# Loads at the start moved between queues, and one tile's routing products moved behind product 3

## The reference

```python
def block0(x, slot):                    # slot: one of the adapters, per sequence
    c = x @ W0.T + b0 + 2 * ((x @ A[slot]) @ B[slot])        # rank 16
    h = silu(c @ W_gate.T) * (c @ W_up.T)                    # 1376 wide
    return h @ W_down.T

def block1(x, lang):                    # two layers, each: base + two of eight experts
    g1 = top2_softmax(x @ Wr.T + 5 * onehot(lang))
    y = x @ W1.T + 2 * sum_e g1[e] * (x @ A1[e].T) @ B1[e].T
    g2 = renormalised_top2(softmax(y @ Wr2.T))
    return y @ W2.T + b2 + 2 * sum_e g2[e] * (y @ A2[e].T) @ B2[e].T

x = x + block0(x, itok_B_0_23)
x = x + block1(x, itok_B_0_7)
```

## Time and profile before

| | |
|---|---|
| median of three runs | 988.67 us (988.07 to 990.8) |
| the profiled execution: time, span | 988.7 us, 986.9 us |
| TensorE matmuls busy | 979.6 us, 99% of the span |
| VectorE, ScalarE, GpSimd busy | 60%, 47%, 26% |
| TensorE's granted clock | full in every slice of the span |
| DMA over the span | 233 GB/s |

### The profile page before, as it was taken

How to read it: one execution, slowest core, us unless ns; L and a number is a source line. 1 busy time by engine, 2 the same in 40 slices (tenths; PEclk the granted TensorE clock), 3 DMA queues, 4 the chain that set the end, 5 groups by cost and what they waited for, 6 DMA issues and landing times.

```text
span 986.9 us, 14042 instructions
## 1 busy us (share of the span) xinstructions
PE 979.6 (99%) x4787; PEld 829.0 (84%) x4787; DVE 591.9 (60%) x969; ACT 464.3 (47%) x854; POOL 256.5 (26%) x244
## 2 busy tenths in 40 slices
PE   8999999999999999999999999999999999999998
PEld 7888888888888888888888888888888899888886
DVE  5654586788784423596333299233278488786762
ACT  5645566555761333572333374233357264535342
POOL 5232232654400631400531230171140460000000
PEclk9999999999999999999999999999999999999999
DMA  8997866666977976877887786986789650606132
GB/s 279 359 321 285 310 215 233 250 224 246 340 268 257 293 222 196 268 224 259 298 277 197 225 269 235 316 281 194 195 268 324 235 193 22 234 33 224 65 107 86
DMA packets 121487, 230.12 MB, mean 233 GB/s; under 512 B 12613, under 2 KB 12613, under 8 KB 121161
## 3 DMA queue, kind: packets, MB, share of 16 engines
q1 hardware_dynamic: 118880, 220.81, 67.1%
q0 software_dynamic: 2400, 8.41, 2.3%
q10 hardware_dynamic: 136, 0.01, 0.0%
HBM read 165.74 MB, written 63.44 MB: 232 GB/s over the span
## 4 chain that ended last, share of the span: by engine, by line
PE 94%; DVE 2%; DMA 2%; issue 1%; ACT 1%; POOL 0%; DVEq 0%; SPq 0%; ACTq 0%
PE bank L1820 92%; DMA ab<-in_ab_table,row_i 1%; PE bank L1844 1%; PE bank L1981 1%; DMA t_raw<-t_scratch 1%; ACT xs_hi L1126 0%; DMA slot_i<-in_slots 0%; DVE hg L1644 0%; DVE greater L1624 0%; DVE xs_lo L1529 0%; ACT bank L1277 0%; DVE wins L1620 0%; DVE rank L1627 0%; DVE greater L1618 0%; POOL ab L776 0%
## 5 line engine op out<-in xcount | busy, mean ns | idle before, releaser
L1820 PE MATMUL bank<-cop_hi,wring 128*128 128x512 f32 x1234 | 380.7, 389 | 0.3 <-issue 0.3
L1820 PEld LDWEIGHTS bank<-cop_hi,wring 128*128 128x128 f32 x1234 | 231.6, 188 | 49.0 <-ACT bank L1041 0.9
L1820 PE MATMUL bank<-cop_lo,wring 128*128 128x512 f32 x616 | 239.7, 389 | 0.0
L1820 PE MATMUL bank<-op_hi,wring 128*128 128x512 f32 x560 | 173.7, 389 | 0.0
L1472 DVE TENSOR_TENSOR v<-bank,p7s 128x512 f32<-128x512 f32 x44 | 30.4, 691 | 200.3 <-PE bank L1820 200.3
L1820 PEld LDWEIGHTS bank<-cop_lo,wring 128*128 128x128 f32 x616 | 115.6, 188 | 23.9
L1820 PEld LDWEIGHTS bank<-op_hi,wring 128*128 128x128 f32 x560 | 105.1, 188 | 21.9
L1820 PE MATMUL bank<-op_lo,wring 128*128 128x512 f32 x280 | 108.9, 389 | 0.0
L1072 ACT ACTIVATE s<-bank 128x512 f32<-128x512 f32 x44 | 26.3, 597 | 115.7 <-PE bank L1820 115.7
L1458 DVE TENSOR_TENSOR op_lo<-h,op_hi 128x512 fp32r<-128x512 f32 x100 | 72.6, 743 | 3.9 <-ACT op_hi L1029 3.7
L821 POOL TENSOR_TENSOR h_t<-h,h 128x512 f32<-128x512 f32 x20 | 27.6, 1382 | 160.4 <-DVE h L1494 160.4
(11 more groups left out here) (227 smaller groups left out, 1926.0 us busy)
## 6 DMA issues: line engine op xcount, KB each, us to landing
wring<-wgu_scratch SPq DMA_DIRECT2D x231, 256.0 KB, 3.0
wring<-wd_scratch SPq DMA_DIRECT2D x140, 256.0 KB, 5.2
wgu_scratch<-wring SPq DMA_DIRECT2D x77, 256.0 KB, 3.6
x_raw<-in_x SPq DMA_DIRECT2D x32, 256.0 KB, 7.3
c_scratch<-c_out SPq DMA_DIRECT2D x32, 256.0 KB, 2.8
c<-c_scratch SPq DMA_DIRECT2D x32, 256.0 KB, 4.2
xs_raw<-x_scratch SPq DMA_DIRECT2D x16, 512.0 KB, 5.7
out<-res SPq DMA_DIRECT2D x32, 256.0 KB, 2.1
```

The costliest lines, as they stand in the source:

```text
L1820: return e.matmul(out_ap, lhs, rhs, start=start, stop=stop, skip_group_check=True)
```

## The change

Three edits, all of place. The load of `w0_raw[0]` goes from SyncE's list to the head of ScalarE's, where the load of `slot_i` stood. The load of `slot_i` goes to the head of GpSimd's program. In the last stage, `route_x` of the second next tile stands behind product 3 for every u; `route_x` of the first next tile stays where it was. For u = 0 nothing changes there.

```diff
@@ sync_program
         for k in range(KC):
             load_x(0, [k])
-            e.dma_start(w0_raw[:, k, :], w0[:, k, :]).then_inc(w0_in[k], DMA)
+            if k > 0:
+                e.dma_start(w0_raw[:, k, :], w0[:, k, :]).then_inc(w0_in[k], DMA)
@@ pool_program
+        e.dma_start(slot_i[:, :], slots.unsqueeze(1).to_broadcast([GB, R, n_batch // GB])).then_inc(slots_in, DMA)
         e.iota(part_i[:, :], [[0, 1]], base=0, channel_multiplier=1).then_inc(pool_const, 1)
@@ act_program
-        e.dma_start(slot_i[:, :], slots.unsqueeze(1).to_broadcast([GB, R, n_batch // GB])).then_inc(slots_in, DMA)
+        e.dma_start(w0_raw[:, 0, :], w0[:, 0, :]).then_inc(w0_in[0], DMA)
         split_x(0)
@@ pe_program
                     if mp == 0 and more and i == (3 if u == 0 else 4):
                         route_x(a + 2)
+                    if mp == 0 and more and i == 3:
                         route_x(b + 2)
```

## The result

The changed kernel takes 991.52 us (median of 8 runs, 990.26 to 992.07), the kernel before 988.60 (8 runs): the ratio is 1.0025, 95% interval 1.0014 to 1.0036. It is slower by 2.5 us by the ratio and 2.9 by the medians, where 1.4 us less were forecast, and lies outside the range. The profiled execution has 990.77 us with a span of 989.0.

The account below looks back on a forecast made before the run. TensorE, busy 979.6 of 986.9 us, was taken to set the pace behind the start's chain of slots and gathers. Start 0.3 and last stage 1.1 off 988.7 gave 987.3 us (45%), range 986.0 to 989.4 (94%).

Parts of the forecast that it names:

- What bounds the kernel: Whole kernel: TensorE busy 979.6 of 986.9 us; gains only from the 7.3 us left, useless work in front, or late matmuls.
- Part 1: Start, w0's first chunk by ScalarE's queue: first product 0 to 1.03 us earlier, 0.5 taken; alone worth 0 to 0.2.
- the 4.46 of the bound: Start: if x and w0 loads share 197 GB/s, both land at 4.46 us, first product at 6.60, no gain.
- Part 2: Start, slots' numbers by GpSimd: landing 0.1 to 0.5 us earlier; 0.3 taken for the second gather's landing at 13.03.
- Part 3: Last stage, second tile's routing behind product 3: removes two waits for the split of x, gain 2 x 0.55 = 1.1 us.
- The slack behind it: Last stage: transposes that reuse the banks keep 2 us to spare after ScalarE's last copy slips; expected cost nothing.
- Rival 2: Start: GpSimd's transfer slow among large loads, slots at 5.2, second gather at 14.4; kernel 989.0 to 989.6 us; 12%.
- Rival 1: Start gives nothing or 0.4 back, since the DMA backlog sets the gathers' landing; 987.6 to 988.0 us; 20%.
- Rival 3: Start: both limits give way, second queue shortens the slow phase before 5 us, up to 1.0 earlier; 986.6 us; 15%.
- Rival 4: Last stage: the routing move doesn't pay, a new wait of the same size for bank or router; 988.4 us; 8%.

## Why the prediction was wrong

**What bounds the kernel**: right. The time moved with the start and the two late waits and with little else. One more stall belongs to no edit: `ACT bank L1043`, 0.5 us, which ends at 211.8 us, after ScalarE had waited for a load of gate weights and for GpSimd; the profile of the last-stage edit's second timing has one of 0.4 there, with the start of before.

**Part 1**: right in its pessimistic end. Both loads shared the rate; x was split from 4.41, w0's load took 3.8 us from 0.81, both close to the 4.46 of the bound. Where VectorE was free the first product stood at 6.81, against 6.57 before: no gain. I took 0.5 of the 0 to 1.03. The term itself cost nothing; but the part said that ScalarE loses one issue and gains another "at nothing", and the issue that it loses is that of the slots.

**Part 2** is the step that failed, three times over. First the duration: I took 2.5 to 2.8 us for the slots' landing from GpSimd's small loads of the kernel before, whose issues stand at 9.6 us and later. In the place where the edit puts the load it took 5.5. SyncE's last large load had been issued 5.4 us ahead of those rows (at 4.21). Two stretches of the kernel before show what they met; the last two numbers are the DMA share and the GB/s:

```profile
9.60:10.90 1.30, 1.30 (x6) 1.08 (x7) 1.30 (x3) 0.86 (x2) 1.30 (x4) 1.00 1.03 419
11.50:12.00 0.50, 0.50 (x4) 0.42 (x3) 0.00 (x0) 0.05 (x1) 0.03 (x1) 1.00 0.23 62
```

The engines were still full when these loads were issued and nearly idle when they landed (at 12.1 the first): they met the end of the backlog, the slots its beginning. A row from the right place was there: SyncE's w0 load, issued at 1.26 and so only 0.45 us behind the first, needed 3.8 us, and even that is short of 5.5. The issue itself I put at 0.8 to 0.92; it was at 1.36 and lasted 0.82. Second, who waits: I followed `slot_i` to the gather and never asked what stands behind `row_i` in VectorE's list, which is the first split. The earlier trace rows show VectorE idle for 2.23 us ahead of `row_i`; I read that as room, where it was a wait at the head of a list. The run with the other order measures it, clock included, at 2.3 us. Third, the clock: nothing in the prediction says what an idle stretch in front does to the matmuls after it, though nine warm-up matmuls stand in front of the first product.

**Part 3**: right in mechanism and size. 0.56 and 0.54 us in the trace, 1.1 in all; 1.6 and 0.6 us by the ratios of the two timings. The slack behind it held.

**The rivals.** Rival 2 named the mechanism, a GpSimd transfer that waits in the large loads' backlog, and the point from which it decides, a landing later than 4.9 us. The landing was at 6.91. Its price was too small: it had 5.2 for the landing, it priced only the gather (989.0 to 989.6), and with VectorE's order mended that is what was measured, 989.1. That agreement is in part luck: the slots came 3.0 us later and not 1.4, and the gather made good more than half of it. The 2.3 us more are VectorE's list and the clock. Rival 1 gave the backlog as the reason that nothing is gained; it made things worse instead. Alone, both paths took 2.4 us; by the Trainium skill, "DMA: Bandwidth & Descriptors", section "Specifications", GpSimd's has the slower first byte, which these two runs do not show. W0 on ScalarE's queue landed 5.7 us after issue, behind SyncE's loads; with this agrees the Trainium skill, "DMA: Bandwidth & Descriptors", section "Issuing engines are not separate DMA queues", by which loads that different engines start run on the same DMA engines. Rival 3 did not occur. Rival 4 fell.

In numbers: the last-stage edit -1.1 (trace), the late gathers +1.3 (the run with VectorE's order mended, +0.2, less that), VectorE's list with the clock +2.3; together the 2.5 us of the ratio. The last two terms are differences of that ratio and so must close; the check that does not hang on it is the one of the two traces above, 2.2 against 2.1 us.

## What to carry to other kernels

In this start, where many loads are issued at once, a load that was issued later landed much later, and a queue of its own did not help; a small load that others wait for is best issued first, and moving it from the head of one list to another cost 2.5 us and more, where its issue came 0.46 to 0.55 us later. The order of issue is not the whole rule: with the slots alone by GpSimd fewer large loads were ahead of them than in the change, and they landed 1 us later. When a load may land later, go through the in-order list of the engine that waits for it and price everything behind the waiting instruction, not only what reads the data. And price an idle stretch of TensorE twice: for itself, and for the clock of the matmuls behind it; filling it with useless matmuls up to the first operands was cheap here. Read a clock of 1.00 at the start of a trace together with the distance of the matmuls' starts.

## What the runs showed of the hardware

A 256 KB load took 3.8 us from issue at 1.26 us and 5.7 us from issue at 2.08, on another queue that held only the slots; 8 KB took 2.4 us alone, 3.0 when issued with the first large load, 4.6 at 1.27 behind one on its own queue, and 5.5 to 6.6 by GpSimd at 1.36. GpSimd's 2 KB and 16 KB took 2.5 and 2.8 us when issued at 9.6 us and later, at the end of the backlog.

TensorE's clock: in every profile the warm-ups began at 1.53 us and stood 0.43 us apart, from the second on, until the clock came up. With nothing but matmuls in front it came up at 6.72, 7.16 and 7.54 us; with nine warm-ups and then idle time at 4.66 to 6.45, and in two executions only at 10.28 and 14.57, behind the first products. Where it came up so early and TensorE stood still behind the warm-ups for 2.0 to 3.9 us, it fell to the lower level in all five profiles (the change, either half of the start alone, both runs with the slots alone on the queues), between 8.07 and 9.86 us. Where TensorE stood still for 0.8 to 1.2 us (before, the last-stage edit's first timing, VectorE's other order) or not at all (12, 19 and 23 warm-ups) it did not. Ahead of the first entry of the clock in a trace the row of a stretch reads 1.00 whatever the pace is.
